# A graph layer on one core: inputs issued in order of need, the identity made on the chip, edge set-up in four parts, duplicate search later, a layer norm's arithmetic on VectorE

## The chip, the cores and the metric

The kernel runs on one NeuronCore of one Trainium2 chip. The metric is device time in microseconds for one execution, lower is better. Times below are us from the start of the profiled span unless marked ns.

## The reference

```
xn = layernorm(x)                              # x: 384 x 1024
x  = x + gnn(xn, src, dst, type) + mix(xn)     # both read the same xn
gnn: q,k,v = xn @ wq.T.. ; q2,k2,v2 = q @ wiq.T.. ; 16 heads of 64
     mask[src, dst] = softplus(w)[type - 1]    # 6144 edges, last one wins; diagonal filled
     softmax(q2 k2' / 8 + mask) v2 @ wo.T
mix: qkv = xn @ Wqkv; qp = elu(q)+1; kp = elu(k)+1
     attn = qp (kp' v) / (qp sum(kp));  y = layer_norm(xn + attn) * g1 + b1
     layer_norm(y + Wd(silu(y Wg) * (y Wu))) * g2 + b2
x  = layernorm(x); out = x + moe(x)            # 8 experts, one per token
```

## The kernel before, in words

All matrix products are in float32 precision, made of three passes. Each operand is split into a rounded high part and the remainder (low part); the products high x high, high x low and low x high are accumulated. `raw` has four slots of 128 x 1024 weights ("a quarter"), `wsp` the two parts of each. For each quarter SyncE's queue issues the load (`load`, which waits until the slot's former content is split: `w_lo`), ScalarE writes the high part (`prep` in its block, the copy at L591, counted by `w_hi`), VectorE the low part (`prep` in its block, through `lo`, L912, counted by `w_lo`), and TensorE uses it (`feature_major`, L1506: 24 matmuls of 128x384 into one of two accumulators, after waits for `w_lo` and for `acc_free`, the release of that accumulator two quarters ago).

Order of the first half. The rows of x are loaded, VectorE takes their statistics (L929, L931), GpSimd makes the reciprocal deviation (`rstd`, L465, L466), VectorE normalises (L944), TensorE transposes (L1535, 24 transposes with `ident`, which lies in the first 128 columns of the loaded table `cst`), ScalarE (L606) and VectorE (L912) write the high and low parts of the transposed x to `feat[0]`. Then come quarters 0 to 15, the query and key projections of the mixing branch. After each of them ScalarE and VectorE make elu+1 (`elu_step`: ScalarE L623 Exp and L624 Relu; VectorE L1002, which also frees the accumulator; each engine then preps the quarter two ahead, and splits the result, L630 and L912). Then 8 token-major quarters (L1520), the products L1557 and L1571/L1576 (the numerators, three token tiles), and 24 quarters for the graph branch's q, k, v (three rounds of 8, L1506). After them tokens are transposed again (L1592) once `x1_done` says that the normed mixing rows `x1` are ready.

Beside this runs the edge work. GpSimd issues the small loads (`small_loads`: edge columns `ei`, type weights `tw`, router tables, the triangle mask `later`). VectorE computes softplus of the type weights with two ScalarE activations (Exp L610, Ln L612, tables are switched for the Ln and back), and then the values and keys of all edges in `ef` (L967 to L976, 12 small instructions of 128x48). Edges are handled in 16 pieces. GpSimd makes the codes of a piece's edge rows (`codes_step`, L492, L494, two buffers, rows loaded by SyncE's queue), VectorE searches the piece for later duplicates (`piece`, L984, L991, L993), GpSimd scatters it (L509, three indirect DMAs, after those of the piece before have landed). In the end the table is loaded as the mask (L513). Pieces sit in VectorE's order in `elu_step` of every even step (0 to 7), after every second prep of the token-major quarters (8 to 11), and ahead of each of the three parts of L1557 and after them (12 to 15). The mixing branch's first layer norm is GpSimd's: after the scatter it loads two rows (`load_row`), and for each token tile runs L465, L466 and three 128x1024 operations (L525 to L527).

All engines run in program order; a wait at the head of a queue holds everything behind it.

## Time and profile before

| what | us |
|---|---|
| median of 3 runs | 637.99 (637.88 to 639.61) |
| the profiled execution's own time | 641.52 |
| its span, first to last instruction | 639.8 |
| TensorE busy in the span | 569.8 (89%) |
| VectorE, ScalarE, GpSimd busy | 458.3, 318.3, 177.2 |
| mean granted TensorE clock | 0.964 of full speed |

The span is what the trace shows; 1.7 us of the profiled execution lie around it. The profiled execution took 3.5 us (0.6%) more than the median.

### The profile page before, as it was taken

How to read it: one execution, taken by the hardware profiler on the slowest of the kernel's cores; microseconds unless marked ns; L12 is line 12 of the kernel's file. 1: busy time of each engine (PE TensorE's matmuls, PEld its weight loads, DVE VectorE, ACT ScalarE, POOL GpSimd, SP SyncE). 2: the span in 40 equal slices, each digit the busy share in tenths (PEclk: the TensorE clock that was granted, in tenths of full speed). 3: DMA queues.
4: the chain of work that ended last, by engine and by line, in shares of the span. 5: the costliest groups of instructions: out<-in, count | busy, mean ns of one | idle time of the engine just before them, and what ended most of it. 6: DMA issues, size and time to landing. Idle time of an engine off the chain costs nothing.

```text
span 639.8 us, 9211 instructions
## 1 busy us (share of the span) xinstructions
PE 569.8 (89%) x3090; PEld 519.7 (81%) x3090; DVE 458.3 (72%) x807; ACT 318.3 (50%) x475; POOL 177.2 (28%) x167
## 2 busy tenths in 40 slices
PE   3699999999999999999999998999898769888970
PEld 2699997888999999999889888899786657766750
DVE  6678887885455444735679899787879655999972
ACT  3445553320333333534366655675653345998960
POOL 5556765856399000710001022100001100000001
PEclk9889999999999999999999999999899959999986
DMA  8356558450533433395322443422662212999936
GB/s 298 134 189 181 171 155 245 115 130 1 183 120 129 164 125 122 107 277 141 96 81 83 105 98 99 105 98 69 228 198 84 80 34 89 330 413 411 412 109 211
DMA packets 33043, 102.69 MB, mean 161 GB/s; under 512 B 5392, under 2 KB 9552, under 8 KB 33008
## 3 DMA queue, kind: packets, MB, share of 16 engines
q1 hardware_dynamic: 27792, 90.02, 41.8%
q0 software_dynamic: 4912, 11.46, 6.8%
q10 hardware_dynamic: 304, 0.79, 0.4%
q8 instruction: 18, 0.29, 0.2%
q14 instruction: 17, 0.14, 0.1%
HBM read 96.65 MB, written 5.60 MB: 160 GB/s over the span
## 4 chain that ended last, share of the span: by engine, by line
PE 53%; DVE 27%; ACT 8%; DMA 6%; issue 5%; POOL 1%; DVEq 0%; ACTq 0%; SPq 0%; POOLq 0%
PE ps L1506 31%; DVE wsp L912 7%; DVE big L912 4%; PE ps L1520 4%; DMA raw<-in_w_experts 3%; PE ps L1685 3%; PE ps L1576 2%; ACT work L712 2%; PE ps L1639 2%; PE ps L1775 2%; PE ps L1614 2%; ACT wsp L591 2%; DVE work L984 2%; DVE pt L912 2%; PE ps L1827 1%
## 5 line engine op out<-in xcount | busy, mean ns | idle before, releaser
L1506 PE MATMUL ps<-big,wsp 128*128 128x384 f32 x1680 | 304.2, 339 | 9.2 <-DVE wsp L912 6.6
L1506 PEld LDWEIGHTS ps<-big,wsp 128*128 128x128 f32 x1680 | 294.4, 190 | 14.0 <-DVE wsp L912 6.4
L912 DVE TENSOR_TENSOR wsp<-raw,wsp 128x1024 fp32r<-128x1024 f32 x117 | 149.9, 1292 | 29.4 <-ACT wsp L591 23.3
L591 ACT ACTIVATE wsp<-raw 128x1024 fp32r<-128x1024 f32 x83 | 87.2, 1053 | 33.5 <-PE ps L1520 12.9
L509 POOL DMA_INDIRECT edge_table<-ef,eidx x48 | 57.4, 1195 | 31.9 <-DMA edge_table<-ef,eidx 19.1
L465 POOL TENSOR_SCALAR rs<-mv 128x1 f32<-128x1 f32 x12 | 9.3, 779 | 199.5 <-DVE mv L1232 102.3
L598 ACT ACTIVATE big<-ps,bias 128x384 f32 x24 | 14.0, 583 | 83.0 <-PE ps L1506 83.0
L923 DVE SCALAR_TENSOR_TENSOR big<-ps,bias,big 128x384 f32 x24 | 14.8, 618 | 51.7 <-ACT big L598 49.7
L912 DVE TENSOR_TENSOR big<-raw_x,big 128x1024 fp32r<-128x1024 f32 x36 | 42.0, 1214 | 0.3 <-ACT big L763 0.3
L763 ACT ACTIVATE wsp<-raw 128x1024 fp32r<-128x1024 f32 x34 | 34.5, 1049 | 7.0 <-DMA raw<-in_w_experts 4.3
L1827 PE MATMUL ps<-wsp,big 128*128 128x512 f32 x112 | 28.8, 399 | 9.6 <-DVE big L912 9.6
L763 ACT ACTIVATE big<-raw_x 128x1024 fp32r<-128x1024 f32 x36 | 36.0, 1046 | 0.1
L712 ACT ACTIVATE work<-work,snm 128x384 f32<-128x384 f32 x48 | 28.9, 604 | 12.7 <-DVE snm L1132 12.7
L1827 PEld LDWEIGHTS ps<-wsp,big 128*128 128x128 f32 x112 | 20.5, 188 | 16.8 <-DVE big L912 12.6
L1520 PE MATMUL ps<-wsp,big 128*128 128x512 f32 x144 | 33.1, 390 | 0.3 <-DVE wsp L912 0.3
L562 POOL DMA_DIRECT2D slot_y<-maskb x7 | 3.8, 545 | 103.3 <-DVE maskb L1414 103.3
L1520 PEld LDWEIGHTS ps<-wsp,big 128*128 128x128 f32 x144 | 26.9, 188 | 6.3 <-DVE wsp L912 0.8
L984 DVE SCALAR_TENSOR_TENSOR work<-codes,ef,maskb 128x384 f32<-128x384 int32 (+2 forms) x48 | 21.8, 502 | 7.3 <-POOL codes L494 7.3
L1639 PE MATMUL ps<-pt,vp 128*128 128x384 f32 x96 | 20.4, 347 | 5.6 <-DVE pt L912 5.4
L1128 DVE CUSTOM_DVE_ANT_0 work<-ps,maskb 128x384 f32<-128x384 f32 x48 | 24.1, 565 | 0.9 <-issue 0.9
L1639 PEld LDWEIGHTS ps<-pt,vp 128*128 128x128 f32 x96 | 16.4, 188 | 8.9 <-issue 8.4
L728 ACT ACTIVATE low_rows<-ps 64x384 f32<-64x384 f32 x16 | 7.8, 489 | 31.5 <-PE ps L1639 31.4
(245 smaller groups left out, 847.5 us busy)
## 6 DMA issues: line engine op xcount, KB each, us to landing
raw<-in_w_stream SPq DMA_DIRECT2D x85, 512.0 KB, 3.5
raw<-in_w_experts SPq DMA_DIRECT2D x32, 512.0 KB, 6.5
raw_x<-in_w_experts SPq DMA_DIRECT2D x32, 512.0 KB, 6.8
rowbuf<-in_rowb POOLq DMA_DIRECT2D x6, 512.0 KB, 6.8
raw_x<-in_w_stream SPq DMA_DIRECT2D x4, 512.0 KB, 6.5
slot_y<-maskb POOLq DMA_DIRECT2D x7, 256.0 KB, 5.6
tok<-in_x SPq DMA_DIRECT2D x3, 512.0 KB, 4.4
edges_a<-in_src_rows SPq DMA_DIRECT2D x8, 192.0 KB
```

Of the source, the lines that this page charges most:

```text
L509: pool.indirect_dma_start(out=table, out_offset=bass.IndirectOffsetOnAxis(ap=eidx[:, c:c + 1], axis=0), in_=ef[:, 3, c:c + 1], in_offset=N ...
L591: nc.scalar.activation(wsp[:, 0, slot, :], raw[:, slot, :], ACT.Copy).then_inc(w_hi, 1)
L712: nc.scalar.activation(probs[:, s, t, :], probs[:, s, t, :], ACT.Exp, bias=snm[:, s, t:t + 1], scale=DH ** -0.5, accum_out=ssum[:, s, t:t ...
L763: nc.scalar.activation(split_of(slot, 0), raw_slot(slot), ACT.Copy).then_inc(w_hi, 1)
L912: return nc.vector.tensor_tensor(dst, value, hi.bitcast(F32), ALU.subtract)
L984: ins = nc.vector.scalar_tensor_tensor(out=into[k], in0=codes[buf][:, k * P:N], scalar=ef[:, 0, bass.ds(c + k, 1)], in1=maskb[:, k, k * P: ...
L1128: ins = nc.vector.tensor_tensor_reduce(out=probs[:, s, t, :], in0=ps[:, 2 + 3 * s + t, 0:N], in1=maskb[:, t, :], scale=1.0, scalar=3.0 * N ...
L1506: ins = nc.tensor.matmul(ps[:, bank, 0:N], wsp[:, a, slot, k * P:(k + 1) * P], moving[:, b, k, :], start=(k == 0 and n == 0), stop=(k == K ...
L1520: ins = nc.tensor.matmul(ps[:, banks + t, :], stationary[:, b, k, t * P:(t + 1) * P], wsp[:, a, slot, kk * HALF:(kk + 1) * HALF], start=(k ...
L1639: ins = nc.tensor.matmul(ps[:, bank, 0:N], vp[:, mt, s, :], pt[:, b, mt, :], start=(mt == 0 and b == 0), stop=(mt == NT - 1 and b == 1))
L1685: ins = nc.tensor.matmul(ps[:, 2 + 3 * h + t, :], feat[0][:, b, k, t * P:(t + 1) * P], split_of(slot_of(Q_WO + h * RING + j), a)[:, kk * H ...
L1827: ins = nc.tensor.matmul(ps[:, bank, :], htk[:, e % 2, k, :], split_of(base + j, a)[:, kk * HALF:(kk + 1) * HALF], start=(k == 0 and a == ...
```

## The change

The x rows and the first two weight quarters are issued first, then the bias columns and the constants without the identity, which GpSimd writes (memset and `affine_select`). The transposes wait for `ident_set` alone. The first quarter's matmuls run pass by pass, so that high x high waits only for the high part of x. Both splitting engines prep quarters 1 to 3 directly after x; the preps ahead in elu steps 0 and 1 fall away. The Ln moves behind elu step 0 on ScalarE, the 12 edge instructions are laid behind steps 0, 1, 2 and 3 on VectorE. Router tables get a semaphore of their own (`route_in`, awaited at the routing). Piece 0 comes in step 4 (was step 0), pieces 2n in steps 4 + 2n; pieces 6 to 9 go with the token-major quarters, 10 and 11 behind the first two numerator tiles, 12 to 15 with every second quarter of the q projection. SyncE's queue is written out for these quarters with the piece loads at named places. VectorE does the layer norm of x1 in two instructions a tile (`x1_scaled`, `x1_shifted`) behind the first six quarters of the v projection; GpSimd keeps `rstd`.

```diff
-            sp.dma_start(cst[:], consts).then_inc(const_in, 16)
-            sp.dma_start(bias[:], cols).then_inc(const_in, 16)
...
             for q in range(RING):
                 load(q * P, q, None)
+                if q == 1:
+                    sp.dma_start(bias[:], cols).then_inc(const_in, 16)
+                    sp.dma_start(cst[:, P:NCONST], consts[:, P:NCONST]).then_inc(const_in, 16)
             for j in range(2):
                 load_piece(j * N, j, None)
-            with sp.Fori(0, (Q_MV - RING) // RING) as i:
+            piece_with = {9: 2, 10: 3, 11: 4, 13: 5, 15: 6, 17: 7, 19: 8, 21: 9, 24: 10, 26: 11, 28: 12, 30: 13,
+                          31: 14, 32: 15}
+            for q in range(RING, Q_GK + RING):
+                load(q * P, q % RING, q - RING + 1)
+                n = piece_with.get(q)
+                if n is not None:
+                    load_piece(n * N, n % 2, n - 1)
+            with sp.Fori(0, (Q_PAIR0 - Q_GK) // RING - 1) as i:
                 for j in range(RING):
-                    row = sp.snap(i * (RING * P) + (RING + j) * P)
-                    load(row, j, i * RING + (j + 1))
-                    if j % 2 == 0:
-                        first = sp.snap(i * (2 * N) + (2 + j // 2) * N)
-                        load_piece(first, j // 2, i * 2 + (j // 2 + 1))
-            for q in range(Q_MV, Q_GQ + RING):
-                load(q * P, q % RING, q - RING + 1)
-                if q % 2 == 0 or q >= Q_GQ:
-                    n = (q - Q_MV) // 2 + 8 if q < Q_GQ else q - Q_GQ + 12
-                    load_piece(n * N, n % 2, n - 1)
-            assert n == PIECES - 1
-            with sp.Fori(0, (Q_PAIR0 - Q_GQ) // RING - 1) as i:
-                for j in range(RING):
-                    row = sp.snap(i * (RING * P) + (Q_GQ + RING + j) * P)
-                    load(row, j, i * RING + (Q_GQ + j + 1))
+                    row = sp.snap(i * (RING * P) + (Q_GK + RING + j) * P)
+                    load(row, j, i * RING + (Q_GK + j + 1))
...
-                pool.dma_start(sbias[:], rowb[R_SW, 0:NT * EXPERTS].partition_broadcast(P)).then_inc(edge_in, 16)
-                pool.dma_start(swt[:], switch_w).then_inc(edge_in, 16)
                 pool.dma_start(maskb[:], later).then_inc(later_in, 16)
+                pool.dma_start(sbias[:], rowb[R_SW, 0:NT * EXPERTS].partition_broadcast(P)).then_inc(route_in, 16)
+                pool.dma_start(swt[:], switch_w).then_inc(route_in, 16)
             then(nc.gpsimd.memset(half[:], -0.5))
             then(nc.gpsimd.memset(width[:], N))
+            then(nc.gpsimd.memset(ident, 0.0))
+            nc.gpsimd.affine_select(out=ident, in_=ident, compare_op=ALU.not_equal, fill=1.0, base=0,
+                                    pattern=[[-1, P]], channel_multiplier=1).then_inc(ident_set, 1)
...
-            pool.wait_ge(const_in, 32)
+            pool.wait_ge(ident_set, 1)
...
             pool.wait_ge(tm_sum, 2 * NT)
             load_row(R_G1, 0)
             load_row(R_B1, 1)
-            pool.wait_ge(rowb_in, rows_in.value)
             for t in range(NT):
                 rstd(t, NT + t)
-                pool.wait_ge(rstd_done, NT + t + 1)
-                row = tok[:, t, :]
-                then(nc.gpsimd.tensor_scalar(row, row, mv[:, t, 0:1], rs[:, t, 1:2], ALU.subtract, ALU.mult))
-                then(nc.gpsimd.tensor_tensor(row, row, rowbuf[:, 0, :], ALU.mult))
-                nc.gpsimd.tensor_tensor(row, row, rowbuf[:, 1, :], ALU.add).then_inc(x1_done, 1)
             pool.wait_ge(x1_done, NT)
...
-            prep(1)
+            for j in range(1, RING):
+                prep(j)
...
             act.wait_ge(tw_arg, 1)
             nc.scalar.activation(tw[:, 1, :], tw[:, 1, :], ACT.Exp).then_inc(tw_exp, 1)
-            act.wait_ge(tw_one, 1)
-            nc.scalar.activation(tw[:, 1, :], tw[:, 1, :], ACT.Ln).then_inc(tw_ln, 1)
...
-                elu_step(j, j)
+                elu_step(j, j, j >= 2)
                 elu_hi_part(1, j)
+                if j == 0:
+                    act.wait_ge(tw_one, 1)
+                    nc.scalar.activation(tw[:, 1, :], tw[:, 1, :], ACT.Ln).then_inc(tw_ln, 1)
...
-            dve.wait_ge(edge_in, 96)
+            for j in range(1, RING):
+                prep(j)
+            dve.wait_ge(edge_in, 64)
...
-            dve.wait_ge(tw_ln, 1)
-            then(nc.vector.scalar_tensor_tensor(out=tw[:, 2, :], in0=tw[:, 0, :], scalar=0.0, in1=tw[:, 1, :],
-                                                op0=ALU.max, op1=ALU.add))
-            nc.vector.tensor_scalar(tw[:, 3, :], tw[:, 2, :], DH ** 0.5, None, ALU.mult).then_inc(tw_done, 1)
-            dve.wait_ge(tw_done, 1)
...
+            def edge_weights():
+                dve.wait_ge(tw_ln, 1)
+                then(nc.vector.scalar_tensor_tensor(out=tw[:, 2, :], in0=tw[:, 0, :], scalar=0.0, in1=tw[:, 1, :],
+                                                    op0=ALU.max, op1=ALU.add))
+                nc.vector.tensor_scalar(tw[:, 3, :], tw[:, 2, :], DH ** 0.5, None, ALU.mult).then_inc(tw_done, 1)
+                dve.wait_ge(tw_done, 1)
+            def edge_start():
+                then(nc.vector.scalar_tensor_tensor(out=ef[:, 0, :], in0=ei[:, 0, :], scalar=float(N), in1=ei[:, 1, :],
+                                                    op0=ALU.mult, op1=ALU.add))
+                then(nc.vector.tensor_scalar(ef[:, 2, :], spare, 1.0, None, ALU.mult))
+                then(nc.vector.tensor_tensor(ef[:, 2, :], ef[:, 2, :], ef[:, 0, :], ALU.subtract))
+            def edge_kind(k, w):
...
-            dve.wait_ge(later_in, 16)
             elu_turn = {q_no: RING, acc: RING, parts: 2 * RING, elus: RING, pieces: 2, edges: 2, step: 2}
             for j in range(RING):
-                elu_step(1, j, j, j // 2 * GROUP)
+                elu_step(1, j, j, j >= 2)
+                if j == 0:
+                    edge_weights()
+                if j == 1:
+                    dve.wait_ge(const_in, 32)
+                    edge_start()
+                    edge_kind(0, 3)
+                if j == 2:
+                    edge_kind(1, 0)
+                    edge_kind(2, 1)
+                if j == 3:
+                    edge_kind(3, 2)
+                    edge_kind(4, 3)
+                    dve.wait_ge(later_in, 16)
...
+                    elu_step(1, i * RING + (RING + j), j)
+                    if j % 2 == 0:
+                        piece(j // 2, j // 2 * GROUP, junk)
...
-                        n = 8 + 2 * h + j // 2
+                        n = 6 + 2 * h + j // 2
...
-                piece(mt % 2, (12 + mt) * GROUP, late_junk)
                 acc_part(pt[:, 1, mt, :], pt[:, 0, mt, :], everyone, 0.0)
-            piece(1, 15 * GROUP, late_junk)
...
+                if t < 2:
+                    piece(t, (10 + t) * GROUP, late_junk)
+            def projection(n, m, j, b0):
+                acc_part(feat[1 + n][:, 1, bass.ds(m, 1), :], feat[1 + n][:, 0, bass.ds(m, 1), :],
+                         everyone, bias[:, bass.ds(m + b0, 1)])
+                prep((j + 2) % RING)
+            def x1_scaled(t):
+                dve.wait_ge(rowb_in, 32)
+                row = tok[:, t, :]
+                then(nc.vector.scalar_tensor_tensor(out=row, in0=row, scalar=mv[:, t, 0:1], in1=rowbuf[:, 0, :],
+                                                    op0=ALU.subtract, op1=ALU.mult))
+            def x1_shifted(t):
+                dve.wait_ge(rstd_done, NT + t + 1)
+                row = tok[:, t, :]
+                nc.vector.scalar_tensor_tensor(out=row, in0=row, scalar=rs[:, t, 1:2], in1=rowbuf[:, 1, :],
+                                               op0=ALU.mult, op1=ALU.add).then_inc(x1_done, 1)
+            with repeat(dve, 2, {**turn, pieces: 2, edges: 2, step: 2}) as i:
+                for j in range(RING):
+                    projection(0, i * RING + j, j, B_Q)
+                    if j % 2:
+                        piece(j // 2, i * (2 * GROUP) + (12 + j // 2) * GROUP, late_junk)
+            with repeat(dve, 2, turn) as i:
+                for j in range(RING):
+                    projection(1, i * RING + j, j, B_K)
+            dve.wait_ge(stats_done, 2 * NT)
+            for m in range(KT):
+                projection(2, m, m % RING, B_V)
+                if m < 2 * NT:
+                    if m % 2:
+                        x1_shifted(m // 2)
+                    else:
+                        x1_scaled(m // 2)
...
-            pe.wait_ge(const_in, 32)
+            pe.wait_ge(ident_set, 1)
...
+            bank = open_acc()
+            def one_pass(a, b, first, last):
+                for k in range(KT):
+                    ins = nc.tensor.matmul(ps[:, bank, 0:N], wsp[:, a, 0, k * P:(k + 1) * P], feat[0][:, b, k, :],
+                                           start=(first and k == 0), stop=(last and k == KT - 1))
+                    if first and k == 0:
+                        ins.then_inc(w_started, 1)
+                return ins
+            pe.wait_ge(w_hi, 1)
+            pe.wait_ge(tr_hi, NT)
+            one_pass(0, 0, True, False)
+            pe.wait_ge(w_lo, 1)
+            one_pass(1, 0, False, False)
             pe.wait_ge(tr_free, NT)
-
-
-            for m in range(1):
-                for j in range(RING):
-                    feature_major(j, feat[0])
+            one_pass(0, 1, False, True).then_inc(acc_ready, 1)
+            q_no.add()
+            for j in range(1, RING):
+                feature_major(j, feat[0])
...
+            dve.wait_ge(route_in, 32)
             dve.wait_ge(logits_ready, 1)
```

## Rows read from the trace of the kernel before

**Rows 1.** The page's first line.

```profile
span 639.8 us, 9211 instructions
```

**Rows 2.** Timeline of TensorE: start, duration, engine, line, operation, tiles, count [idle before <- releaser].

```profile
8.76 4.95 PE L1535 MATMUL ps<-cst,tok 128*128 128x128 f32 x24 [8.76 <-DMA bias<-in_cols]
16.19 10.16 PE L1506 MATMUL ps<-big,wsp 128*128 128x384 f32 x48 [2.47 <-DVE big L912]
31.53 15.29 PE L1506 MATMUL ps<-big,wsp 128*128 128x384 f32 x72 [5.17 <-DVE wsp L912]
47.08 16.92 PE L1506 MATMUL ps<-big,wsp 128*128 128x384 f32 x96 [0.27 <-DVE wsp L912]
...
208.87 50.20 PE L1506 MATMUL ps<-big,wsp 128*128 128x384 f32 x288 [0.64 <-DVE wsp L912]
258.91 2.78 PE L1592 MATMUL ps<-cst,tok 128*128 128x128 f32 x24
```

**Rows 3.** Busy time by window: window, length, each engine, granted clock, DMA.

```profile
17.50:18.00 0.50, 0.50 (x4) 0.50 (x3) 0.00 (x0) 0.00 (x0) 0.43 (x2) 0.50 1.09 394
...
32.00:34.00 2.00, 2.00 (x8) 2.00 (x8) 1.93 (x10) 0.00 (x0) 0.00 (x0) 0.50 0.64 211
```

**Rows 4.** Timeline of all engines, up to the first quarter.

```profile
7.16 0.76 DVE L944 TENSOR_SCALAR tok<-tok,mv,rs 128x1024 f32<-128x1024 f32 x1
...
9.96 1.06 ACT L591 ACTIVATE wsp<-raw 128x1024 fp32r<-128x1024 f32 x1 [7.87 <-DMA raw<-in_w_stream]
...
10.79 0.81 DVE L944 TENSOR_SCALAR tok<-tok,mv,rs 128x1024 f32<-128x1024 f32 x1 [0.76 <-POOL rs L466]
...
12.66 3.48 DVE L912 TENSOR_TENSOR big<-ps,big 128x1024 fp32r<-128x1024 f32 x3
...
12.86 0.54 POOL L454 DMA_DIRECT2D tw<-in_type_weights  x1
...
13.75 1.03 ACT L606 ACTIVATE big<-ps 128x1024 fp32r<-128x1024 f32 x1 [0.25 <-PE ps L1535]
...
16.05 1.21 DVE L912 TENSOR_TENSOR wsp<-raw,wsp 128x1024 fp32r<-128x1024 f32 x1
```

**Rows 5.** Timeline of all engines, 20 to 32 us: edge set-up and the first ELU.

```profile
20.07 0.17 DVE L957 TENSOR_SCALAR tw<-tw 128x4 f32<-128x4 f32 x1 [2.80 <-DMA swt<-in_switch_w]
...
22.27 1.28 ACT L623 ACT_TABLE_LOAD   x1
...
23.57 0.58 ACT L623 ACTIVATE work<-ps,bias 128x384 f32<-128x384 f32 x1
...
26.48 0.72 DVE L975 TENSOR_SCALAR ef<-cst 128x48 f32<-128x48 f32 x1
...
27.24 1.04 DVE L976 TENSOR_TENSOR ef<-ef 128x48 f32<-128x48 f32 x1
...
28.32 1.22 DVE L1002 SCALAR_TENSOR_TENSOR work<-work,row_buf 128x384 f32<-128x384 f32 x1
...
29.46 2.02 DVE L912 TENSOR_TENSOR wsp<-raw,wsp 128x1024 fp32r<-128x1024 f32 x1
```

**Rows 6.** DMA issues, 0 to 60 us: size each, us from issue to landing.

```profile
tw<-in_type_weights POOLq DMA_DIRECT2D x1, 2.0 KB, 5.5
```

**Rows 7.** Timelines of GpSimd and VectorE, 143 to 209 us.

```profile
143.48 0.99 POOL L509 DMA_INDIRECT edge_table<-ef,eidx  x1 [4.64 <-DMA edge_table<-ef,eidx]
...
165.25 0.81 POOL L513 DMA_DIRECT2D maskb<-edge_table  x1 [1.46 <-DMA edge_table<-ef,eidx]
...
197.82 4.58 POOL L525 TENSOR_SCALAR tok<-tok,mv,rs 128x1024 f32<-128x1024 f32 x1
...
201.71 1.23 DVE L912 TENSOR_TENSOR wsp<-raw,wsp 128x1024 fp32r<-128x1024 f32 x1
...
205.87 2.87 DVE L912 TENSOR_TENSOR wsp<-raw,wsp 128x1024 fp32r<-128x1024 f32 x1
```

**Rows 8.** Groups of VectorE instructions by line and shape, whole span.

```profile
L1169 DVE SCALAR_TENSOR_TENSOR tok<-tok,mv,rowbuf 128x1024 f32<-128x1024 f32 x3 | 3.8, 1279 | 0.0
```

More of the change, by code:

```diff
@@ L960, in _ @@
             nc.vector.tensor_scalar(tw[:, 1, :], tw[:, 1, :], 1.0, None, ALU.add).then_inc(tw_one, 1)
-            dve.wait_ge(tw_ln, 1)
-            then(nc.vector.scalar_tensor_tensor(out=tw[:, 2, :], in0=tw[:, 0, :], scalar=0.0, in1=tw[:, 1, :],
-                                                op0=ALU.max, op1=ALU.add))
-            nc.vector.tensor_scalar(tw[:, 3, :], tw[:, 2, :], DH ** 0.5, None, ALU.mult).then_inc(tw_done, 1)
-            dve.wait_ge(tw_done, 1)
-            then(nc.vector.scalar_tensor_tensor(out=ef[:, 0, :], in0=ei[:, 0, :], scalar=float(N), in1=ei[:, 1, :],
-                                                op0=ALU.mult, op1=ALU.add))
-            for k, w in ((0, 3), (1, 0), (2, 1), (3, 2), (4, 3)):
+            def edge_weights():
[10 more added lines that the diff above has]
+            def edge_kind(k, w):
                 dst = ef[:, 3, :] if k == 0 else ef[:, 1, :]
@@ L994, in piece, with elu_step @@
                 edges.add()
-            def elu_step(big, m, j, c):
+            def elu_step(big, m, j, ahead=True):
                 acc.add()
```

29 lines of the change are left out of this document (11 added, 18 removed).

## The prediction

> **What bounds the kernel now.** I read the totals first: TensorE is busy for nine tenths of the span [rows 1], so only its idle time, and stretches in which it runs slow, can be won in a few microseconds. TensorE's timeline gives them in order [rows 2]. It starts its transposes at 8.76, when the last of the constants has landed; it starts the first quarter at 16.19; it finishes two quarters at 26.35 and idles 5.17 until 31.53; from then on, up to 209, its waits on VectorE are a few tenths each, apart from one of 1.2 ahead of the numerators that the change doesn't touch. So the stretch to 31.5 is bounded by latencies: VectorE and ScalarE in program order, not matmul work. After it TensorE is the bound, at 50.20 / 288 = 0.174 a matmul, 4.2 a quarter.
>
> The windows add a second loss [rows 3]. The granted clock stands at 0.50 (1.2 GHz of 2.4) at 17.5, after the idle time before 16.19, and again at 32 to 34, after the 5.17. The cost is read from rows at either level: the 72 matmuls from 31.53 took 15.29 where 72 x 0.174 = 12.5 would do, so 2.8. The two quarters from 16.19 took 10.16 instead of 8.4, so 1.8. The 24 first transposes took 4.95, those of 258.91 took 2.78 [rows 2]: the beginning runs at the slow level too, whatever the page's clock line says there.
>
> Why does the third quarter wait? Its accumulator is free, but its weights come late: VectorE reaches that split (row 29.46) only after the type weights, the twelve edge instructions and the first ELU addition [rows 5]. Its first edge instruction waited until 20.07 for `swt`, a router table that nothing needs before the routing. ScalarE is no better off; it does Exp and Ln with two table loads before the first ELU, at 23.57.
>
> **The beginning, step by step.** The first x tile is normalised at 7.92, the third at 11.60 [rows 4]. With the identity made by two short GpSimd instructions in the idle time before the statistics, the first eight transposes start at 7.95. At the slow rate (4.95 / 24 = 0.206 each, 1.65 a tile) the three tiles end at 9.6, 11.7 and 13.35; before, 13.71. The third tile is now held by its normalisation, so 0.8 at the start becomes 0.36. ScalarE: raw 0 landed at 9.96 behind the constants and is now issued one microsecond earlier with 343 KB fewer ahead of it, so its copy is done by about 10.1 and delays no x copy. The third x copy is 13.4 to 14.4. VectorE is unchanged to 16.14 (end of the 3.48 row). Before, the first quarter waited for that; now its 8 + 8 matmuls on the high part of x start at 14.45 and last 16 x 0.174 = 2.8 at least, so the low part is there when it is wanted. **Gain at the first quarter: 16.19 - 14.45 = 1.7.**
>
> **Quarters 1 to 3.** ScalarE copies three slots at 1.05 each, 14.4 to 17.6; VectorE splits them at 1.21 each (row 16.05), 16.14 to 19.8. So quarters 1, 2 and 3 have weights before TensorE wants them (at 18.7, 22.9, 27.1 at the fast rate, later at the slow one). The limit is now the accumulator, hence the ELU steps. Type weights were issued at 12.86 and land 5.5 later [rows 4, 6], 18.4, before VectorE is free at 19.8; its two small operations end at 20.2. ScalarE: Exp of the weights to 20.45, then ELU 0, two activations at 0.58 overlapping to 1.1, to 21.5. VectorE's addition (0.55 where GpSimd is idle) frees accumulator 0 at 22.1, in time for quarter 2. The high part goes to 22.7. Ln and its table, and the load back before ELU 1, take 1.30 + 0.2 + 1.30 (from 22.27 to 23.57 in [rows 5]), to 25.5. ELU 1 ends 26.6, accumulator 1 is free at about 27.2: quarter 3 waits 0.1 if TensorE is fast all along, nothing otherwise.
>
> **Quarter 4** needs accumulator 0 again and a split of its own in step 2, behind step 1's rest on VectorE. The low part of ELU 1 ends at 28.5. `edge_start` and the first kind follow: 0.24 + 0.76 + 1.08 + 0.28 with gaps, 2.4 (I keep the long durations of rows 26.48 and 27.24, because GpSimd's code arithmetic falls here as it did there), to 30.9. Then the addition, 1.1 (between the quiet 0.55 and the 1.22 of row 28.32), and the split, 1.4 (between 1.21 and 2.02), to 33.3. By TensorE alone, with the slow stretch of the first two quarters kept, quarter 4 would start at 14.45 + 10.16 + 2 x 4.2 = 33.0; with no slow stretch at 31.3. So 33.3 comes out either way. Before, it started at 31.53 + 15.29 - 4.2 = 42.6 [rows 2]. **Gain: 9.3**, made of 1.7 (start) + 5.2 (idle gone) + 2.8 (no clock loss after it) less 0.3 to 0.4 of new waiting. The remaining edge instructions, four of some 0.35 behind each of steps 2 and 3, lie where pieces of 1.7 lay before, and cost nothing; without that cover step 3's split would be late by their 1.5.
>
> **What is moved later.** Six pieces rather than eight lie beside the ELU steps, and the small waits (0.27 at 47.08) depend on the even steps' pieces, which stay: nothing. Pieces 12 to 15 come with the q projection, where VectorE does 0.62 + 1.23 a quarter of 4.2; a piece of 1.7 fits. SyncE's queue holds a weight load behind a piece load only until `codes_done`; each named place is at or after the step that gives those codes, and a load is issued four quarters (17 us) ahead of its split. The scatter ended before 165.25 [rows 7] and should end about 200 in the same frame; rows G1, B1 follow in 8. The first use is at 232, and the mask is wanted beyond 300. So all this is hidden by 20 or more. VectorE's two norm instructions take 1.28 each [rows 8] behind 2.9 of a 4.2 quarter: they just fit, and x1 is whole some 4 before the second transposes. The next row load starts then and GpSimd's additions come perhaps 2 later than before, hidden by the three quarters of gate, up and down projections.
>
> **GpSimd's norm removed.** Under L525 one split took 2.87 instead of 1.23 [rows 7], and quarter 209 waited 0.64 [rows 2]. That goes: **0.6**.
>
> **Sum.** 9.3 + 0.6 = 9.9. Against the profiled execution 641.5 - 9.9 = 631.6. That one was 3.5 above the median, for reasons no row separates, so against the median 638.0 - 9.9 = **628.1**. A measurement of this kernel tells about 0.3%, 1.9 us, from no change.
>
> **Rivals.**
> *Faster still* (0.13). The edge instructions are short (some 0.2) because GpSimd is elsewhere, quarter 4 starts at 31.3: 11.3 + 0.6, 626.1; if the small waits of the following steps (1.2 in all) go too, 624.9.
> *The stall moves to quarter 4 and takes the clock with it* (0.13). If the ELU, edge and split chain of steps 1 and 2 is 2.7 longer than I sum, quarter 4 starts at 36 with idle time before it, the clock falls as before 31.53, 1.5 more: gain 5.1 + 0.6, 632.3. For it: both engines are in a chain with no slack from 20 to 33. Against: each term is from a row and I took the long ones.
> *The table switch costs double* (0.04). If each switch held ScalarE for another 1.4, ELU 1 and all behind it would be 2.8 later: 630.9. Against: the activation started 1.30 after its load did [rows 5]. The Trainium skill, "ScalarE: Activation LUTs", section "What ACT_TABLE_LOAD costs", puts a switch at about 2.66 us, half of it a drain. By that rule the time would be that rival's; the row shows no drain, and I go by the row.
> *It doesn't do it* (0.05). ScalarE and VectorE now wait for the type weights ahead of ELU 0. Landing after 19.8 costs one for one; at 29 it eats the gain: 637.4. Against: 5.5 to landing in 0 to 60 us [rows 6], and the bigger weight loads of quarters 5 and 6 now share the engines from 17 on, which is one microsecond of risk rather than nine.
> *Slower* (0.07). Codes late in the q projection: VectorE waits at the head of `piece`, behind it the acc part and split that TensorE needs. A scatter may wait 4.64 for the one before [rows 7], so a turn of GpSimd can reach 10, against 8.4 for two quarters. Past about 1.7 a wait is TensorE's. Four pieces each 4.5 late would lose 4 x 2.8 = 11.2 and more than cancel: 639.3; it decides from 4.2 late each. Against: codes are made one piece ahead, and pieces 9 to 12 are spaced wide.
> The forecast itself has 0.58, its own range 626.0 to 630.8.
>
> **The range.** Faster still and the stall rival lie at 624.9 and 632.3; I take 624.8 to 632.8, which leaves out the last two rivals and the tails of the others. Faster by over 0.3%: 0.58 + 0.13 + 0.13 + 0.04 = 0.88. Same: 0.05. Slower: 0.07.
>
> **What would show it.** In the changed trace: transposes at about 8, the first L1506 at 14.2 to 14.8; no idle time of TensorE over 2 before quarter 4, and that quarter's start near 33; at most one stretch at clock 0.50 between 15 and 40; ELU 0's first activation near 20.5; no wait on codes in the q projection; no long split under GpSimd at 200. Wrong would be: type weights landing after 20, a clock of 0.50 beyond 30, VectorE idle on L494 after 155, or TensorE idle before the second transposes.

## The result, and the profile after

The changed kernel takes 632.14 us (628.23 to 633.39, 4 runs) against 638.0 (637.88 to 639.61, 4 runs): a ratio of 0.9885, 95% interval 0.985 to 0.9919, so 5.9 us faster. Forecast were 628.1 and a range of 624.8 to 632.8. Timed again in another job, it took 630.83 against 638.57, a ratio of 0.9877 (0.9846 to 0.9908). The size of the gain was overestimated by 2 to 4 us, its sign was right. The first median lies in the range, 0.7 from its slow end, and outside the 626.0 to 630.8 that the forecast itself had. The profiled execution of the changed kernel is one at 632.16, with a span of 630.3.

TensorE's timeline of the changed kernel (start, duration, engine, line, operation, tiles, count, idle time before and who ended it) answers to [rows 2]:

```profile
7.93 1.94 PE L1579 MATMUL ps<-cst,tok 128*128 128x128 f32 x8 [7.93 <-DVE tok L940]
10.05 3.68 PE L1579 MATMUL ps<-cst,tok 128*128 128x128 f32 x16 [0.18 <-DVE tok L940]
14.93 4.40 PE L1585 MATMUL ps<-big,wsp 128*128 128x384 f32 x24 [1.21 <-ACT big L599]
19.17 8.48 PE L1550 MATMUL ps<-big,wsp 128*128 128x384 f32 x48
28.20 4.40 PE L1550 MATMUL ps<-big,wsp 128*128 128x384 f32 x24 [0.55 <-DVE work L1002]
34.75 14.32 PE L1550 MATMUL ps<-big,wsp 128*128 128x384 f32 x72 [2.15 <-DVE wsp L908]
...
151.13 100.72 PE L1550 MATMUL ps<-big,wsp 128*128 128x384 f32 x576
251.69 2.78 PE L1650 MATMUL ps<-cst,tok 128*128 128x128 f32 x24
```

The first quarter starts at 14.93 (14.45 forecast), the next two follow without a wait, and the 5.17 of idle time is gone. In its place stand 0.55 ahead of quarter 3 and 2.15 ahead of quarter 4, which starts at 34.75 instead of the forecast 33.3. The 72 matmuls from there take 14.32 where 12.5 would do. The windows show why (window, length, each engine's busy time, granted clock, DMA share, GB/s); they answer to [rows 3]:

```profile
17.50:18.00 0.50, 0.50 (x5) 0.50 (x4) 0.50 (x1) 0.12 (x1) 0.43 (x2) 1.00 0.87 331
...
32.00:34.00 2.00, 0.60 (x4) 0.28 (x2) 1.97 (x3) 1.29 (x3) 1.45 (x2) 1.00 0.00 0
...
36.00:38.00 2.00, 2.00 (x8) 2.00 (x7) 1.97 (x4) 0.52 (x1) 0.00 (x0) 0.50 0.56 221
```

Of the first 60 us, one stretch is still at half the clock, from about 35 to 38, behind the new idle time. From 151 to 252 the 0.64 of [rows 2] is no more. All engines' timeline around steps 0 to 2 answers to [rows 5]:

```profile
20.56 0.17 DVE L951 TENSOR_SCALAR tw<-tw 128x4 f32<-128x4 f32 x1 [0.44 <-DMA tw<-in_type_weights]
...
24.79 1.28 ACT L615 ACT_TABLE_LOAD   x1
...
26.09 0.58 ACT L615 ACTIVATE work<-ps,bias 128x384 f32<-128x384 f32 x1
...
27.23 0.82 DVE L1002 SCALAR_TENSOR_TENSOR work<-work,row_buf 128x384 f32<-128x384 f32 x1 [2.06 <-ACT row_buf L616]
...
28.79 1.16 POOL L491 TENSOR_TENSOR row_buf<-edges_a,width 128x384 int32<-128x384 int32 x1
...
29.20 0.82 DVE L966 SCALAR_TENSOR_TENSOR ef<-ei 128x48 f32<-128x48 int32 x1
...
30.04 1.02 POOL L493 TENSOR_TENSOR codes<-row_buf,edges_a 128x384 int32<-128x384 int32 x1
30.06 1.04 DVE L968 TENSOR_SCALAR ef<-cst 128x48 f32<-128x48 f32 x1
31.13 0.90 POOL L491 TENSOR_TENSOR row_buf<-edges_b,width 128x384 int32<-128x384 int32 x1
31.14 0.21 DVE L969 TENSOR_TENSOR ef<-ef 128x48 f32<-128x48 f32 x1
...
31.38 0.70 DVE L974 TENSOR_SCALAR ef<-ei,tw 128x48 f32<-128x48 int32 x1
32.11 0.56 DVE L1002 SCALAR_TENSOR_TENSOR work<-work,row_buf 128x384 f32<-128x384 f32 x1
...
32.59 2.02 DVE L908 TENSOR_TENSOR wsp<-raw,wsp 128x1024 fp32r<-128x1024 f32 x1
```

The four edge instructions hold VectorE from 29.20 to 32.08, and the split of quarter 4 ends at 34.6. Which of that is program order and which is contention, the experiments had to say. The rows give a hint: the three long ones each end 0.04 to 0.07 after the GpSimd instruction that was running when they began (30.02 after 29.95, 31.10 after 31.06, 32.08 after 32.03). The fourth keeps its 0.21 (31.14), though one of GpSimd's runs beside it.

### The profile page after: what moved, and what is told of

The parts are those of the page before. It is cut to its first block, busy times and chain, and to the rows that moved or that the text cites. A ratio compares the mean times of both kernels' runs of the same rounds, so it can differ in the third digit from the quotient of the medians.

```text
span 630.3 us, 9111 instructions
## 1 busy us (share of the span) xinstructions
PE 565.7 (90%) x3090; PEld 516.0 (82%) x3090; DVE 461.8 (73%) x813; ACT 318.0 (50%) x475; POOL 151.5 (24%) x160
## 4 chain that ended last, share of the span: by engine, by line
PE 57%; DVE 22%; ACT 8%; DMA 6%; issue 5%; POOL 1%; DVEq 0%; ACTq 0%; SPq 0%; POOLq 0%
PE ps L1550 32%; DVE wsp L908 5%; PE ps L1564 5%; DVE big L908 4%; DMA raw<-in_w_experts 3%; PE ps L1743 2%; PE ps L1697 2%; PE ps L1634 2%; ACT work L708 2%; PE ps L1672 2%; PE ps L1835 2%; PE ps L1615 2%; DVE pt L908 2%; PE ps L1887 1%; ACT wsp L584 1%
## 5 line engine op out<-in xcount | busy, mean ns | idle before, releaser
L1550 PE MATMUL ps<-big,wsp 128*128 128x384 f32 x1656 | 297.3, 337 | 4.0 <-DVE wsp L908 3.3
L1550 PEld LDWEIGHTS ps<-big,wsp 128*128 128x128 f32 x1656 | 287.6, 189 | 8.6 <-issue 5.1
L508 POOL DMA_INDIRECT edge_table<-ef,eidx x48 | 55.8, 1161 | 31.9 <-DMA edge_table<-ef,eidx 16.7
L919 DVE SCALAR_TENSOR_TENSOR big<-ps,bias,big 128x384 f32 (+1 forms) x24 | 14.8, 617 | 34.2 <-ACT big L591 33.5
L724 ACT ACTIVATE low_rows<-ps 64x384 f32<-64x384 f32 x16 | 7.8, 489 | 31.3 <-PE ps L1697 31.3
L908 DVE TENSOR_TENSOR pt<-ps,pt 128x1152 fp32r<-128x1152 f32 x16 | 21.6, 1352 | 1.3 <-ACT pt L716 1.2
```

Source lines behind the costliest of these rows:

```text
L508: pool.indirect_dma_start(out=table, out_offset=bass.IndirectOffsetOnAxis(ap=eidx[:, c:c + 1], axis=0), in_=ef[:, 3, c:c + 1], in_offset=N ...
L908: return nc.vector.tensor_tensor(dst, value, hi.bitcast(F32), ALU.subtract)
L919: nc.vector.scalar_tensor_tensor(out=dst, in0=ps[rows, bank, 0:N], scalar=b, in1=hi.bitcast(F32), op0=ALU.add, op1=ALU.subtract).then_inc( ...
L1550: ins = nc.tensor.matmul(ps[:, bank, 0:N], wsp[:, a, slot, k * P:(k + 1) * P], moving[:, b, k, :], start=(k == 0 and n == 0), stop=(k == K ...
```

## The experiments

**The changed kernel again, and the kernel before as a kernel of its own.** No edit.

> The changed kernel once more, timed in five rounds beside the kernel before, with a profile of each. Theory 1 (clock): runs of one kernel differ by how many stretches TensorE spends at the half clock around its idle times, so that times fall into groups 1.7 or 3.4 us apart, and the mean clock of a run goes with its time: about 632.1 at a mean clock of 0.969, about 628.2 at 0.974. Theory 2 (something else, as DMA landing): times spread without the mean clock moving with them. Median 630 to 633 by both, 5.5 to 6.5 under the kernel before.

> The kernel before, unchanged, as a kernel of its own, to have clock and span of several of its runs. My prediction carried the profiled execution's gain over to the median. If that was the failing step, most runs of the kernel before show a mean clock of 0.967 or more and a span near 636.3, and the profiled one (0.964, 639.8) had about two half-clock stretches more than they. Rival: the clock is 0.964 in all, and the 3.5 us lie in waits. Median 638.

The changed kernel: 630.83 us (627.89 to 632.87, 6 runs), against 638.57. The kernel before: 639.04 (635.82 to 640.83, 12 runs), ratio 1.0004 (0.998 to 1.0028). Times go with the mean clock: the changed kernel 627.89 at 0.977, 630.3 to 631.1 at 0.970 to 0.971, 632.87 at 0.966; the kernel before, in the runs beside these, 634.84 at 0.968, about 638 at 0.966, 640.6 to 642.3 at 0.959 to 0.961. So theory 1 holds in direction, though the steps are not clean. The profiled execution of before (0.964, 641.52) was among its longer ones, and the second profile shows where they differ. TensorE's timeline of the kernel before in this second profile:

```profile
16.36 11.41 PE L1506 MATMUL ps<-big,wsp 128*128 128x384 f32 x48 [2.92 <-DVE big L912]
32.93 14.25 PE L1506 MATMUL ps<-big,wsp 128*128 128x384 f32 x72 [5.16 <-DVE wsp L912]
...
142.80 4.37 PE L1576 MATMUL ps<-big,pt 128*128 128x512 f32 x18
```

The loss at the beginning is the same (3.0 and 1.8 where it was 1.8 and 2.8), but the first numerators take 4.37 here and took 5.98 in the first profile, at half clock behind the same 1.17 of idle time. And of the changed kernel, in the profile of this job:

```profile
27.98 4.40 PE L1550 MATMUL ps<-big,wsp 128*128 128x384 f32 x24 [0.33 <-DVE work L1002]
34.53 21.08 PE L1550 MATMUL ps<-big,wsp 128*128 128x384 f32 x120 [2.15 <-DVE wsp L908]
```

Same 2.15 of idle time, no half-clock stretch after it: 21.08 / 120 = 0.176 a matmul. Whether such a wait costs the clock changes from execution to execution.

**Edge blocks one step later.**

```diff
-                if j == 1:
+                if j == 2:
                     dve.wait_ge(const_in, 32)
                     edge_start()
                     edge_kind(0, 3)
-                if j == 2:
-                    edge_kind(1, 0)
-                    edge_kind(2, 1)
                 if j == 3:
+                    edge_kind(1, 0)
+                    edge_kind(2, 1)
                     edge_kind(3, 2)
                     edge_kind(4, 3)
```

> The three start instructions and the first kind of the edge set-up behind step 2 instead of step 1, the four others all behind step 3. Theory 1: in the changed kernel the edge block of step 1 (29.2 to 32.1) holds the ELU addition and the split of quarter 4, TensorE idles 2.15 before quarter 4 and loses another 1.8 to the clock. So here quarter 4 starts at 32.6 or 32.7 without idle time, no row shows clock 0.50 between 33 and 40, and the time falls by 2.2 + 1.8 = 4.0, to about 628.1. Rival: the split of quarter 4 is bound by GpSimd's code arithmetic or ScalarE's copy and not by the edge block; then under 1 us is gained. Second rival: the block only moves the wait to quarter 5, gain about 1.

628.75 us (626.95 to 631.1, 6 runs), ratio 0.9841 (0.9808 to 0.9874). TensorE's timeline:

```profile
27.88 26.01 PE L1549 MATMUL ps<-big,wsp 128*128 128x384 f32 x144 [0.92 <-DVE work L1002]
54.44 16.96 PE L1549 MATMUL ps<-big,wsp 128*128 128x384 f32 x96 [0.55 <-DVE wsp L908]
```

From quarter 3 on there is no wait for six quarters, and no half clock. So the edge block was what held quarter 4. Against the changed kernel in the same job the medians differ by 2.1 (4.0 forecast), an amount that the intervals don't separate. Two things reduce it: in that job's profile of the changed kernel the wait cost its 2.15 alone and no clock, and the later waits are 0.5 here against 0.2 to 0.3 there. By rows the products behind the token-major quarters start at 118.09 here, against 119.51 in that profile and 121.27 in the first one of the changed kernel: 1.4 without the half-clock stretch, 3.2 with it.

**The norm's arithmetic back on GpSimd.**

```diff
             load_row(R_B1, 1)
+            pool.wait_ge(rowb_in, rows_in.value)
             for t in range(NT):
                 rstd(t, NT + t)
+                pool.wait_ge(rstd_done, NT + t + 1)
+                row = tok[:, t, :]
+                then(nc.gpsimd.tensor_scalar(row, row, mv[:, t, 0:1], rs[:, t, 1:2], ALU.subtract, ALU.mult))
+                then(nc.gpsimd.tensor_tensor(row, row, rowbuf[:, 0, :], ALU.mult))
+                nc.gpsimd.tensor_tensor(row, row, rowbuf[:, 1, :], ALU.add).then_inc(x1_done, 1)
...
                 projection(2, m, m % RING, B_V)
-                if m < 2 * NT:
-                    if m % 2:
-                        x1_shifted(m // 2)
-                    else:
-                        x1_scaled(m // 2)
```

> The changed kernel with the first layer norm's arithmetic given back to GpSimd (three 128x1024 operations a tile, after both row loads), and taken from VectorE's v projection. My prediction put the edit at 0.6 us, by one split of 2.87 that made a quarter late. Theory 1: 0 to 0.7 us slower than the changed kernel, with TensorE waits of up to 0.6 in the q to v projections and splits of over 2 us under L525. Rival: it costs nothing, because a quarter has slack enough in the new order. A third: it is faster, because VectorE is freer there.

631.48 us (629.7 to 632.38, 4 runs), ratio 0.9879 (0.9838 to 0.992); 0.65 more than the changed kernel, which the intervals can't tell from nothing. The rows can. VectorE's timeline, and the waits of TensorE from 150 to 262 (us in total, times, longest):

```profile
231.14 3.17 DVE L914 TENSOR_TENSOR wsp<-raw,wsp 128x1024 fp32r<-128x1024 f32 x1 [0.33 <-ACT wsp L590]
```

```profile
PE ps L1551 <- DVE wsp L914: 1.6, 2, 0.9
```

In the changed kernel the same stretch has no wait at all. The edit is worth 1.6 in the new order, more than the 0.6 of the old one. The later pieces have moved GpSimd's nine long instructions from 175 to 208 (before) to 212 to 246. Three splits run long beside them in both, but they take 2.33, 1.43 and 2.87 in the kernel before, and 3.17, 2.98 and 2.01 here; why these are longer no run separates.

**The beginning alone, on the kernel before.** The identity by memset and `affine_select`, its own semaphore, constants and biases behind the second quarter's load, and the first quarter pass by pass, as in the change; of the rest nothing but this wait:

```diff
+            dve.wait_ge(const_in, 32)
             then(nc.vector.tensor_scalar(ef[:, 2, :], spare, 1.0, None, ALU.mult))
```

> The kernel before with the beginning alone: identity made by GpSimd, constants and biases issued behind the second weight quarter, the first quarter pass by pass. Edge set-up, preps, pieces and the layer norm stay. Theory 1: the first quarter starts at 14 to 15 instead of 16.2, but the third still waits for its split behind the edge set-up at 31.3 to 31.6, so the 1.3 us are lost in a longer idle time: 0 to 0.5 us faster than the kernel before. Rival: the start counts in full, 1.3 faster. Second rival: the longer idle time costs one more stretch at the half clock, 1.7 slower.

639.13 us (636.04 to 642.42, 12 runs), ratio 1.0008 (0.998 to 1.0037): nothing gained. TensorE's timeline:

```profile
14.53 4.40 PE L1547 MATMUL ps<-big,wsp 128*128 128x384 f32 x24 [1.21 <-ACT big L611]
18.77 4.32 PE L1512 MATMUL ps<-big,wsp 128*128 128x384 f32 x24
32.05 14.94 PE L1512 MATMUL ps<-big,wsp 128*128 128x384 f32 x72 [8.96 <-DVE wsp L917]
```

The first quarter starts 1.7 earlier, two quarters end 3.3 earlier (23.1 for 26.35; half of that is that they take 8.6 in this execution and took 10.16 in that one), and all of it goes into an idle time of 8.96. An earlier start counts only with what comes behind it.

**Early preps alone, on the kernel before.** Both engines:

```diff
-            prep(1)
+            for j in range(1, RING):
+                prep(j)
...
-                elu_step(1, j, j, j // 2 * GROUP)
+                elu_step(1, j, j, j // 2 * GROUP, j >= 2)
```

> The kernel before, with quarters 1 to 3 prepped right behind x on both engines and no preps in ELU steps 0 and 1, nothing else. Theory 1: the weights are ready, and the third quarter now waits for its accumulator: the ELU addition comes behind the edge set-up, at 28.5 to 29.6, so it starts near 29.6 instead of 31.5, and the clock still falls: 1.5 to 2.5 us faster. Rival: weights were the wait, and it goes wholly: 5 or more faster. Second rival: the wait returns a quarter later, nothing gained.

637.27 us (634.88 to 642.41, 12 runs), ratio 0.9974 (0.9947 to 1.0): about 1.2 faster, at the edge of what can be told. TensorE's timeline:

```profile
30.70 15.55 PE L1508 MATMUL ps<-big,wsp 128*128 128x384 f32 x72 [4.34 <-DVE work L1003]
```

The third quarter starts 0.8 earlier than in the kernel before, not 1.9 as expected: the router table that the type weights' operations wait for lands at 21.09 instead of 20.07, and all behind them moves by that. The releaser is now the ELU addition (L1003), not a split: the accumulator has become the limit, as the prediction's section on quarters 1 to 3 has it, and the edge set-up still stands ahead of that.

**The edge set-up unsplit.**

```diff
+            edge_weights()
+            dve.wait_ge(const_in, 32)
+            edge_start()
+            for k, wt in ((0, 3), (1, 0), (2, 1), (3, 2), (4, 3)):
+                edge_kind(k, wt)
+            dve.wait_ge(later_in, 16)
             for j in range(RING):
                 elu_step(1, j, j, j >= 2)
-                if j == 0:
-                    edge_weights()
...
```

with the Ln ahead of ELU step 0 on ScalarE.

> The changed kernel with the edge set-up again in one block ahead of ELU step 0 (Ln ahead of it too); beginning, early preps, later pieces and norm on VectorE stay. Theory 1: the block (5.6 us in the kernel before) holds the first ELU addition to 28.5 to 29.5, the third quarter starts there instead of at 23.4, TensorE idles over 5 us and loses the clock; 4 to 6 us slower than the changed kernel, about 635.5. Rival: what was gained is due to the early preps and later pieces, and the split is worth under 1.5.

634.43 us (630.51 to 637.93, 10 runs), ratio 0.9922 (0.9889 to 0.9956), 2.3 to 3.6 slower than the changed kernel in its two jobs; the intervals of the ratios still overlap a little (from 0.9889 here, to 0.9919 and 0.9908 there), so the rows have to carry it. TensorE's timeline:

```profile
27.95 31.62 PE L1542 MATMUL ps<-big,wsp 128*128 128x384 f32 x168 [5.14 <-DVE work L1001]
```

The third quarter starts at 27.95 (23.4 with the split), behind 5.14 of idle time. The releaser is the ELU addition behind the block. The four to six forecast were too many by the medians, because with the block over early the next seven quarters run without a wait. By rows the products behind the token-major quarters (L1607) start at 123.83, against 121.27 and 119.51 in the two profiles of the changed kernel: 2.6 and 4.3.

**Ln behind step 1 as well.** On top of the later edge blocks:

```diff
-                if j == 0:
+                if j == 1:
                     act.wait_ge(tw_one, 1)
                     nc.scalar.activation(tw[:, 1, :], tw[:, 1, :], ACT.Ln).then_inc(tw_ln, 1)
...
-                if j == 0:
+                if j == 1:
                     edge_weights()
```

> The kernel with the edge blocks one step later (behind steps 2 and 3), and the Ln with its two table loads and the last type weight operations behind ELU step 1 instead of 0. Theory 1: the wait of 0.3 to 0.9 ahead of quarter 3 is ELU 1 held by the two table loads (2.8 us on ScalarE); behind step 1 they lie in time in which ScalarE waits for quarter 2. Quarter 3 starts at 27.0 without a wait, quarter 4 at 31.4: 0.9 faster than the version with late edge blocks alone (628.75), about 627.9. Rival: the loads now hold ELU 2 and quarter 4's copy, and the wait moves there: no change or up to 1 slower.

631.47 us (626.75 to 633.13, 6 runs), ratio 0.9864 (0.9821 to 0.9906): no better than the changed kernel, and not the 627.9 expected. Timeline of TensorE, then of all engines:

```profile
31.96 4.43 PE L1549 MATMUL ps<-big,wsp 128*128 128x384 f32 x24 [0.82 <-DVE wsp L908]
37.77 17.04 PE L1549 MATMUL ps<-big,wsp 128*128 128x384 f32 x96 [1.37 <-DVE wsp L908]
```

```profile
33.88 0.83 POOL L491 TENSOR_TENSOR row_buf<-edges_b,width 128x384 int32<-128x384 int32 x1
33.89 0.85 DVE L968 TENSOR_SCALAR ef<-cst 128x48 f32<-128x48 f32 x1
```

Quarter 3 no longer waits, so the table loads were its cause. But type weights, hence GpSimd's codes, came 1.8 later, met the later edge block, and the wait returned, 0.82 ahead of quarter 4 and 1.37 ahead of quarter 5: the second part of the rival. It also pointed at the codes.

**Codes of pieces 0 and 1 first.** GpSimd makes them before it waits for the type weights:

```diff
-            pool.wait_ge(ident_set, 1)
-            pool.wait_ge(tw_done, 1)
-            then(nc.gpsimd.tensor_scalar(diag[:], ident, tw[:, 3, 3:4], None, ALU.mult))
...
             for j in range(2):
                 codes_step(j, None)
+            pool.wait_ge(ident_set, 1)
+            pool.wait_ge(tw_done, 1)
+            then(nc.gpsimd.tensor_scalar(diag[:], ident, tw[:, 3, 3:4], None, ALU.mult))
...
             pool.wait_ge(table_out, 16)
```

> The changed kernel with GpSimd's codes of pieces 0 and 1 (four 128x384 integer operations) ahead of its wait for the type weights instead of behind the table's store. Theory 1: the edge block of step 1 is long (2.9 us for four instructions of 128x48, one of 0.21 where GpSimd is idle) because GpSimd's codes run beside it, and the split of quarter 4 takes 2.02 instead of 1.22 for the same cause. Without them the block takes 1.0 to 1.3, the split 1.2, quarter 4 starts by 32.8 instead of 34.6, its idle time is under 0.5 and no half-clock stretch follows: 2 to 4 us faster than the changed kernel, 627 to 629. Rival: the instructions are long because of the table's store or DMA traffic at that time, and they stay long: quarter 4 as before. Second rival: the codes now slow preps 2 and 3 or ELU 0, and as much is lost there.

628.04 us (627.02 to 631.44, 6 runs), ratio 0.9827 (0.9788 to 0.9866). Timelines of TensorE and of all engines:

```profile
29.33 25.20 PE L1550 MATMUL ps<-big,wsp 128*128 128x384 f32 x144 [0.94 <-DVE work L1002]
```

```profile
30.25 0.20 DVE L966 SCALAR_TENSOR_TENSOR ef<-ei 128x48 f32<-128x48 int32 x1
30.49 0.19 DVE L968 TENSOR_SCALAR ef<-cst 128x48 f32<-128x48 f32 x1
...
30.71 0.21 DVE L969 TENSOR_TENSOR ef<-ef 128x48 f32<-128x48 f32 x1
30.96 0.25 DVE L974 TENSOR_SCALAR ef<-ei,tw 128x48 f32<-128x48 int32 x1
31.24 0.56 DVE L1002 SCALAR_TENSOR_TENSOR work<-work,row_buf 128x384 f32<-128x384 f32 x1
31.71 1.22 DVE L908 TENSOR_TENSOR wsp<-raw,wsp 128x1024 fp32r<-128x1024 f32 x1
```

The same four instructions, at the same place in VectorE's order, take 1.0 instead of 2.9, the split 1.22 instead of 2.02, and quarters 3 to 8 run in one piece. This is theory 1, by rows, with quarter 4 at 33.6 (32.8 expected). The table's store is issued at 29.07, right ahead of the block, so it is not the cause. Quarter 4's wait thus needed both, the edge block in step 1 and the codes beside it; moving either one takes it away. The second rival shows too: the codes now slow the type weights' operation (0.74 for 0.17) and ELU 0, and quarters 2 and 3 wait 0.45 and 0.94 (nothing and 0.55 in the changed kernel). The first numerators start at 132.99, against 134.04 and 135.80 in the two profiles of the changed kernel. It is the fastest median of all twelve, but its interval still overlaps that of the changed kernel.

**Edge and type loads ahead of the statistics.**

```diff
-            def small_loads():
+            def edge_loads():
                 for k, r in enumerate((src_cols, dst_cols, type_cols)):
                     pool.dma_start(ei[:, k, :], r).then_inc(edge_in, 16)
                 pool.dma_start(tw[:, 0, :], type_weights.partition_broadcast(P)).then_inc(edge_in, 16)
+
+            def small_loads():
...
                                     pattern=[[-1, P]], channel_multiplier=1).then_inc(ident_set, 1)
+            edge_loads()
```

> The changed kernel with the edge columns' and type weights' loads issued by GpSimd right behind the identity, ahead of the reciprocal deviations. Theory 1: the type weights then land before 12, VectorE goes on at 19.8 to 20.1 without a wait, and ELU 0, ELU 1, the edge block and quarter 4 all come 0.2 to 0.6 earlier: 0.2 to 0.6 us faster, not to be told from no change by the median, but to be read in the rows. Rival: GpSimd is held by the four issues past the first statistics, or the loads delay the third x tile: the first transposes or the first quarter start later, up to 1 us slower.

632.04 us (629.17 to 634.5, 6 runs), ratio 0.9877 (0.9836 to 0.9918): no gain. Timeline of all engines:

```profile
8.10 1.29 DVE L928 BATCH_NORM_STATS2 stats<-tok 128x6 f32<-128x512 f32 x2 [0.26 <-DMA tok<-in_x]
...
11.07 1.76 DVE L943 TENSOR_SCALAR tok<-tok,mv,rs 128x1024 f32<-128x1024 f32 x1 [0.77 <-POOL rs L468]
```

The third x tile lands 0.26 after VectorE wants it, and its normalisation takes 1.76 instead of 0.81 [rows 4], so the first quarter starts at 16.06, 1.1 later, as the rival had it. Why the normalisation takes so long no row tells. The type weights' wait is gone, and it was worth less.

**Codes first and edge loads first together, with the Ln behind step 1.** `edge_start` behind step 1, kinds 0 and 1 behind step 2, kinds 2 to 4 behind step 3.

> Both of these together, with Ln and the last weight operations behind ELU step 1, the three start instructions behind step 1, kinds 0 and 1 behind step 2 and kinds 2 to 4 behind step 3. Theory 1: no wait ahead of quarters 3, 4 and 5 of more than 0.3, no half-clock stretch between 15 and 60, quarter 4 starts near 31.3: the faster-still case of the prediction for the beginning, 626 to 627.5. Rival: one of the blocks is still long and a wait of 1 or more comes before quarter 5, as with the Ln moved alone: 629 to 631.

631.22 us (628.62 to 633.78, 6 runs), ratio 0.9865 (0.9824 to 0.9906). Waits ahead of quarters 2 to 4 are 0.38, 0 and 0.61, no half clock there, as hoped, but quarter 4 starts at 33.93, not near 31.3: the first quarter starts at 15.79, again behind a long normalisation of the third tile (1.75), and the sum is no better than the changed kernel.

**Router tables awaited again.** Their loads ahead of the mask's, and

```diff
             dve.wait_ge(edge_in, 64)
+            dve.wait_ge(route_in, 32)
```

> The changed kernel with the router tables again loaded ahead of the triangle mask and awaited by VectorE ahead of the type weights' operations (as in the kernel before). Theory 1: they land 0 to 1.4 after the type weights, all that follows moves by that, quarter 4 to 34.7 to 36: 0 to 1.5 us slower than the changed kernel. Rival: it is what the change brought, because the preps don't cover the landing: 2 or more slower.

631.31 us (630.14 to 632.54, 6 runs), ratio 0.9871 (0.9834 to 0.9907). Quarter 4 starts at 34.61, the changed kernel's at 34.75 and 34.53. The semaphore of their own brought nothing that these rows show: with three preps ahead, VectorE goes on at 20.1 with these tables landed too. In the profile of the early preps alone, which has this wait as well, they came 0.94 too late (21.09), so it is worth something in some executions.

## Why the prediction held, and where it was off

*The beginning.* Right in order: identity early, transposes at 7.93, the last copy of x as the limit. Quarter 0 began 1.26 earlier, not 1.7. The third tile was normalised at 11.57, but was not bound by that: the second tile's transposes lasted to about 12.0, because a tile took 1.8 to 1.9, not the 1.65 of the sum. They ended at 13.7, not 13.35, and ScalarE's copy of 1.02 followed, as summed. That rate changes from execution to execution too: in the profiles of the later edge blocks, the norm on GpSimd, the Ln behind step 1 and the unsplit set-up, which leave the beginning as it is, quarter 0 starts at 13.89 to 14.24. The beginning alone is worth nothing (639.13); it was not a separate term, and the sum took it rightly as a part of quarter 4's start.

*Quarters 1 to 3.* Right: no wait ahead of 1 and 2, the accumulator as the new limit (L1002 is the releaser of the 0.55). The type weights came 7.7 after their issue, at 20.54, not at 18.4: the median of [rows 6] was a single landing. That is 0.44 of waiting; in the second profile they took 7.2 and nothing waited. The two table loads behave as summed: the load at 24.79, the activation at 26.09, 1.30 apart. A switch shows no drain here either, and so the rival with the doubled price, which rests on the Trainium skill, "ScalarE: Activation LUTs", section "What ACT_TABLE_LOAD costs", did not come true. As an estimate by that section's figure, quarter 4 would have started 2.8 later than summed; it started 1.45 later, and the rows account for that otherwise.

*Quarter 4, the term that was mis-sized.* Forecast 33.3, measured 34.75; a gain of 42.6 - 34.75 = 7.85 instead of 9.3. The edge block started at 29.2 (28.5 forecast) and took 2.9 (2.4), addition and split together 2.5 (2.5). I did name contention with GpSimd's codes and took the long durations from [rows 5], but took too few of them: three of four instructions were long, not two. What I did not see is that this was no fixed price: moving the codes removes 1.9 of the block and 0.8 of the split.

*The clock.* This is the step where the reasoning failed. I counted the 2.8 behind the old idle time as won, and argued that 33.3 comes out "either way", with or without a slow stretch in the first quarters. The second way leaves TensorE idle ahead of quarter 4, and that idle time can bring its own half-clock stretch: 14.32 - 12.5 = 1.8 in the profiled run. It was my rival of the stall that moves and takes the clock with it: half of its delay (quarter 4 at 34.75, 1.45 later than summed, where the rival had 36 and 2.7) and all of its clock (1.8, where it had 1.5). In four profiles with this wait (the changed kernel twice, norm on GpSimd, router tables awaited) the stretch came twice. So the range held the result because that rival was inside it, and not because the forecast's own sum was right: 9.9 less 1.45 less 1.8 is 6.65, against 7.2 by rows (below).

*The norm.* 0.64 at 208.87 is gone, as forecast. Restoring GpSimd's norm in the new order shows 1.6 of waits.

*What is moved later.* Right: no wait of TensorE from 151 to 252, mask load issued at 201.8 (200 forecast), x1 done at 247.8, and GpSimd's next additions start 1.5 behind the transposes of 251.69. No piece held VectorE on codes there, so no row shows the slower rival.

*From the profile to the median.* Span against span the gain is 639.8 - 630.3 = 9.5, close to 9.9, but for a different reason. Up to the second transposes it is 258.91 - 251.69 = 7.2; the other 2.3 fall behind them, where the change does nothing, and 1.6 of them at the first 18 projection matmuls, before and after:

```profile
459.55 5.99 PE L1685 MATMUL ps<-wsp,big 128*128 128x512 f32 x18 [1.82 <-DVE snm L1132]
```

```profile
452.37 4.35 PE L1743 MATMUL ps<-wsp,big 128*128 128x512 f32 x18 [1.87 <-issue]
```

Over all fourteen profiles (the kernel before, the changed kernel and the twelve runs), this group takes 5.96 to 6.00 in nine and 4.35 to 4.39 in five, behind 1.82 to 1.88 of idle time; the first numerators take 5.94 to 5.99 in eight and 4.33 to 4.37 in six, behind the same 1.17. Kernels with and without the change are on both sides. I had noted the profiled execution's 3.5 above the median as something that no row separates. Against the second profile of the kernel before (span 636.4), 1.6 of its 3.4 more is the numerators' stretch, and the rest falls behind 490, where the change does nothing.

The 7.2 lie between the 5.9 and 7.7 of the two jobs, but they are one pair. The second pair, in which the changed kernel's profile has no half-clock stretch ahead of the second transposes, has 257.34 - 248.32 = 9.0. What the change is worth in one execution thus depends on the clock by some 2 us.

The undone parts do not add up to the whole: beginning alone 0, early preps alone about 1.2, and without the split the whole keeps 4.1 of its 7.7. They lift successive limits of one chain. The later pieces were not taken back in a run by themselves, and neither was the first quarter's pass by pass. What also stays open is what decides, at equal waits, whether the clock falls; no run here separates that.

## What to carry to other kernels

When a stall is removed from a chain with no slack, work out what is late next, and give its own idle time the price of the clock too, not only the old one's. Price a VectorE instruction by what GpSimd does beside it, and ask whether that neighbour could stand elsewhere: here four instructions moved by some eight microseconds took the 2.15 of idle time ahead of quarter 4 away, for 0.45 and 0.39 more ahead of quarters 2 and 3. Take a gain from one profiled pair only up to the last place that the change touches; what differs behind it is not its doing.

## What was not expected of the hardware

- VectorE instructions of 128x48 take 0.20 to 0.25 alone and mostly 0.70 to 1.04 beside GpSimd's 128x384 integer operations, ending just after these do; one beside such an operation keeps its 0.21. A split of 128x1024 takes 1.22 alone, 2.02 beside those, and up to 3.17 beside GpSimd's 128x1024 operations.
- The same idle time of 1.17 or 2.15 of TensorE is followed by the half clock in some executions and not in others; one kernel's runs spread over some 5 to 8 us (634.84 to 642.34 in one job), and the times go with the mean clock, though not in clean steps.
- A 2 KB load by GpSimd's queue took 5.5 and 5.8 to land in the two profiles of the kernel before, and 7.7 and 7.2 in those of the changed kernel, in which more weight loads are under way then. Whether these are the cause no run separates.
